# Feature-major x for two attention batches: the norm's scales and shifts go through DRAM and GpSimd

## The reference, cut to what matters

```python
def _layernorm(x, axis=-1, eps=1e-05):
    m = jnp.mean(x, axis=axis, keepdims=True)
    v = jnp.var(x, axis=axis, keepdims=True)
    return (x - m) / jnp.sqrt(v + eps)

# x: (4, 512, 256); ctx_1024: (4, 512, 256); 16 heads of 64, a causal window of 64
qh = (q @ wq.T).reshape(b, l, H, DH)          # q is _layernorm(x)
kh = (k @ wk.T).reshape(b, l, H, DH)          # k and v are ctx_1024
scores = jnp.einsum('bhqd,bhkd->bhqk', _rope(qh), _rope(kh)) * DH ** (-0.5)
probs = jax.nn.softmax(jnp.where(window_mask, scores, -1e+30), axis=-1)
x = x + jnp.tanh(g_xattn[0]) * (out @ wo.T)
x = x + jnp.tanh(g_ffn[0]) * ffn(_layernorm(x))   # 2 shared and 16 routed experts
```

## Time and profile before

| what | value |
|---|---|
| median of 3 runs | 520.59 us (520.58 to 520.6) |
| the profiled execution's own time | 520.59 us |
| its span in the trace | 518.8 us |
| busy in the span: PE, DVE, ACT, POOL | 504.1 (97%), 362.3 (70%), 311.1 (60%), 256.4 us (49%) |
| granted PE clock | full in all 40 slices |

### The profile page before, as it was taken

How to read it: one execution, slowest core, us unless ns; L and a number is a source line. 1 busy time by engine, 2 the same in 40 slices (tenths; PEclk the granted TensorE clock), 3 DMA queues, 4 the chain that set the end, 5 groups by cost and what they waited for, 6 DMA issues and landing times.

```text
span 518.8 us, 12294 instructions
## 1 busy us (share of the span) xinstructions
PE 504.1 (97%) x4394; PEld 422.6 (81%) x4394; DVE 362.3 (70%) x1165; ACT 311.1 (60%) x859; POOL 256.4 (49%) x198
## 2 busy tenths in 40 slices
PE   8888999899999999999999999999999999999997
PEld 5767798799889989888888888777887888788885
DVE  6868868658756677785978586797657665855454
ACT  3468677466675657756685794774546545544442
POOL 4999997788889778987987730101000100000000
PEclk9999999999999999999999999999999999999999
DMA  7361222111031011201212119314911491166021
GB/s 258 99 170 53 76 77 103 58 37 37 4 118 37 8 33 37 59 7 53 57 42 58 37 50 322 103 31 117 296 23 22 125 287 17 23 153 232 1 33 48
DMA packets 47723, 44.12 MB, mean 85 GB/s; under 512 B 29168, under 2 KB 31472, under 8 KB 47664
## 3 DMA queue, kind: packets, MB, share of 16 engines
q1 hardware_dynamic: 47664, 43.35, 29.8%
HBM read 30.62 MB, written 2.23 MB: 63 GB/s over the span
## 4 chain that ended last, share of the span: by engine, by line
PE 75%; POOL 10%; DVE 7%; issue 4%; ACT 2%; DMA 1%; SPq 0%; DVEq 0%; POOLq 0%; ACTq 0%
PE ring L1017 53%; PE psS L1017 10%; PE psO L1199 4%; PE psT L1180 4%; PE psS L1168 4%; POOL arena L465 3%; POOL arena L467 2%; POOL prob L471 2%; DVE arena L772 1%; POOL wl L479 1%; DVE wl L848 1%; DVE arena L918 1%; POOL arena L458 1%; DVE arena L775 1%; DMA craw<-in_ctx 1%
## 5 line engine op out<-in xcount | busy, mean ns | idle before, releaser
L1017 PE MATMUL ring<-xTh,wh 128*128 128x512 f32 x272 | 110.0, 404 | 1.8 <-DVE wl L848 1.5
L1017 PE MATMUL ring<-xTh,wl 128*128 128x512 f32 x272 | 106.8, 393 | 0.0
L1017 PE MATMUL ring<-xTl,wh 128*128 128x512 f32 x272 | 106.7, 392 | 0.0
L471 POOL TENSOR_TENSOR prob<-prob,rinv 128x512 f32<-128x512 f32 x64 | 68.4, 1069 | 19.4 <-DVE rinv L928 19.4
L566 ACT ACTIVATE oTh<-prob 128x512 fp32r<-128x512 f32 x64 | 40.4, 631 | 54.3 <-PE ring L1017 25.9
L831 DVE TENSOR_TENSOR oTl<-prob,oTh 128x512 fp32r<-128x512 f32 x64 | 43.9, 687 | 35.6 <-ACT oTh L566 35.1
L1017 PEld LDWEIGHTS ring<-xTh,wh 128*128 128x128 f32 x272 | 51.1, 188 | 14.9 <-issue 2.9
L550 ACT ACTIVATE sneg<-ring 128x512 f32<-128x512 f32 x72 | 42.9, 596 | 33.6 <-PE ring L1017 33.5
L490 POOL TENSOR_TENSOR rstd<-vare,mhalf 128x4 f32<-128x4 f32 x8 | 10.1, 1267 | 103.3 <-DVE vare L741 103.3
L641 ACT ACTIVATE pT<-psT 128x512 f32<-128x512 f32 x64 | 38.0, 594 | 38.2 <-PE psT L1180 38.2
L1017 PEld LDWEIGHTS ring<-xTh,wl 128*128 128x128 f32 x272 | 51.1, 188 | 11.3
(11 more groups left out here) (123 smaller groups left out, 1227.5 us busy)
## 6 DMA issues: line engine op xcount, KB each, us to landing
arena<-gate_scratch SPq DMA_DIRECT2D x64, 256.0 KB, 6.5
raw<-in_e SPq DMA_DIRECT2D x18, 256.0 KB, 2.7
raw<-in_w SPq DMA_DIRECT2D x16, 256.0 KB, 3.5
arena<-arena SPq DMA_DIRECT2D x16, 256.0 KB, 3.1
arena<-arena SPq DMA_DIRECT2D x16, 192.0 KB, 3.5
pT<-pT SPq DMA_DIRECT2D x96, 32.0 KB, 2.0
out<-x SPq DMA_DIRECT2D x16, 128.0 KB, 6.0
x<-in_x SPq DMA_DIRECT2D x3, 512.0 KB, 3.7
```

The lines of the kernel that those rows point to most:

```text
L471: pool.tensor_tensor(prob[:, c % BUFS, :, :], prob[:, c % BUFS, :, :], rinv[:, c % BUFS, :].unsqueeze(2).to_broadcast([P, TT, P]), ALU.mul ...
L1017: last = pe.matmul(out, a, b, start=start and i == 0 and j == 0, stop=stop and i == n - 1 and j == 2, skip_group_check=check)
```

## The change

For the batches 2 and 3 (the third and the fourth), x is also loaded from DRAM with the features on the partitions, into the tile `xn` that the normalised x took before. The scale (`rstd`) and shift of each token lie one token to a partition; SP writes them to a DRAM scratch and reads them back spread over all partitions, first the scales and later the shifts, into the tile `idle`. POOL multiplies and adds (two halves each, 128x512). ACT rounds the result to `xTh[0]`, DVE subtracts to `xTl[0]` in two halves. Batch 1 keeps the old way; so do all norms of the experts. The statistics of batches 2 and 3 move from step (k, g) = (3, 1) to step (0, 0) of the batch before.

```diff
+        xd = xn[:, :, :].rearrange("p t d -> p (t d)").rearrange("p (k n) -> p k n", k=KC)
+        xd_tiles = xd.rearrange("p k (t c) -> p k t c", t=TT)
+        by_tile = idle.rearrange("p (c t) -> p t c", t=TT)
+        norm_d = nc.dram_tensor("norm_scratch", (B, 2, L), F32).ap()
...
-            if (k, g) == (2, 2) and b + 1 < B:
-                jobs.append(("xT", b + 1))
-            if (k, g) == (3, 1) and b + 1 < B:
-                jobs.append(("stat", b + 1))
+            if (k, g, b) == (2, 2, 0):
+                jobs.append(("xT", 1))
+            if (k, g, b) == (3, 1, 0):
+                jobs.append(("stat", 1))
+            spread = {(0, 0): "stat", (1, 0): "norm_out", (2, 0): "in_scale", (3, 0): "scale_a", (0, 1): "scale_b",
+                      (1, 1): "in_shift", (3, 1): "shift_a", (0, 2): "shift_b", (2, 2): "xhi_d", (3, 2): "xlo_d"}
+            if 1 <= b < B - 1 and (k, g) in spread:
+                jobs.append((spread[k, g], b + 1))
...
-            if (k, g) == (0, 2) and b + 1 < B:
-                jobs.append(("norm_a", b + 1))
-            if (k, g) == (1, 2) and b + 1 < B:
-                jobs.append(("norm_b", b + 1))
+            if (g, b) == (2, 0) and k < 2:
+                jobs.append(("norm_a" if k == 0 else "norm_b", 1))
...
@@ @block.sync
+                elif kind == "norm_out":
+                    sp.wait_ge(ln_rstd, n + 1)
+                    for i, part in enumerate((rstd, shift)):
+                        sp.dma_start(norm_d[n, i].rearrange("(p t) -> p t", t=TT), part[:, :]).then_inc(norm_out, 16)
+                    if n == 2:
+                        sp.wait_ge(xT_pe, 2)
+                    else:
+                        sp.wait_ge(xT_lo, n)
+                    sp.dma_start(xd, xt_d[n]).then_inc(in_xt, 16)
+                elif kind == "in_scale":
+                    sp.wait_ge(norm_out, 32 * (n - 1))
+                    if n > 2:
+                        sp.wait_ge(x_shifted, n - 2)
+                    sp.dma_start(idle, norm_d[n, 0].partition_broadcast(P)).then_inc(in_scale, 16)
+                elif kind == "in_shift":
+                    sp.wait_ge(x_scaled, n - 1)
+                    sp.dma_start(idle, norm_d[n, 1].partition_broadcast(P)).then_inc(in_shift, 16)
...
@@ @block.gpsimd
+                elif kind in ("scale_a", "scale_b"):
+                    kc = int(kind == "scale_b")
+                    pool.wait_ge(in_xt, 16 * (n - 1))
+                    pool.wait_ge(in_scale, 16 * (n - 1))
+                    scaled = pool.tensor_tensor(xd_tiles[:, kc, :, :], xd_tiles[:, kc, :, :], by_tile, ALU.mult)
+                    if kc:
+                        scaled.then_inc(x_scaled, 1)
+                elif kind in ("shift_a", "shift_b"):
+                    kc = int(kind == "shift_b")
+                    pool.wait_ge(in_shift, 16 * (n - 1))
+                    moved = pool.tensor_tensor(xd_tiles[:, kc, :, :], xd_tiles[:, kc, :, :], by_tile, ALU.add)
...
                 elif kind == "stat":
                     pool.wait_ge(ln_stat, n + 1)
...
@@ @block.scalar
+                elif kind == "xhi_d":
+                    act.wait_ge(x_shifted, n - 1)
+                    act.wait_ge(qk_pe[0], GROUPS * n + 1)
+                    act.activation(xTh[0][:, :, :], xd, ACT.Copy).then_inc(xT_hi, 1)
...
@@ @block.vector
+                elif kind in ("xhi_d", "xlo_d"):
+                    kc = int(kind == "xlo_d")
+                    dve.wait_ge(xT_hi, n + 1)
+                    rest = dve.tensor_tensor(xTl[0][:, kc, :], xd[:, kc, :], xTh[0][:, kc, :].bitcast(F32),
+                                             ALU.subtract)
```

More of the change, by code:

```diff
@@ L59, in products, with build @@
     return ((sh, mh), (sh, ml), (sl, mh))
-def build(nc, x_d, ctx_d, gx_d, gf_d, w_d, e_d, rw_d, cos_d, sin_d, mask_d, ident_d, out_d):
+def build(nc, x_d, xt_d, ctx_d, gx_d, gf_d, w_d, e_d, rw_d, cos_d, sin_d, mask_d, ident_d, out_d):
     with ExitStack() as ctx:
@@ L160, in build @@
         ln_norm = sem("ln_norm")
+        norm_out, in_xt, in_scale, in_shift = sem("norm_out"), sem("in_xt"), sem("in_scale"), sem("in_shift")
+        x_scaled, x_shifted = sem("x_scaled"), sem("x_shifted")
         xT_pe, xT_hi, xT_lo = sem("xT_pe"), sem("xT_hi"), sem("xT_lo")
@@ L289, in released, with by_pe @@
                     "r": (r_sub, n + 1)}[kind]
+        def by_pe(j):
+            return j if j < 2 else j - B + 2
         def fillings(u):
@@ L485, in do @@
                                        ALU.subtract).then_inc(c_lo, 1)
+                elif kind in ("scale_a", "scale_b"):
[9 more added lines that the diff above has]
+                    moved = pool.tensor_tensor(xd_tiles[:, kc, :, :], xd_tiles[:, kc, :, :], by_tile, ALU.add)
+                    if kc:
+                        moved.then_inc(x_shifted, 1)
                 elif kind == "stat":
                     pool.wait_ge(ln_stat, n + 1)
-                    if n:
-                        pool.wait_ge(ln_norm, n)
+                    if n in (3, 4):
+                        pool.wait_ge(norm_out, 32 * (n - 2))
+                    elif n:
+                        pool.wait_ge(ln_norm, by_pe(n - 1) + 1)
                     power = pool.tensor_tensor(rstd[:, :], vare[:, :], mhalf[:, :], ALU.pow)
@@ L534, in round_bank_pair @@
             def round_bank_pair(dst, job, ready, done):
-                act.wait_ge(ready, job[1] + 1)
+                act.wait_ge(ready, by_pe(job[1]) + 1)
                 two = banks(job)
@@ L617, in normalise @@
                 act.wait_ge(ln_rstd, j + 1)
-                act.wait_ge(xT_pe, min(j, B + 2))
+                if j == 1:
+                    act.wait_ge(xT_pe, 1)
+                elif j == B:
+                    act.wait_ge(xT_lo, B)
+                else:
+                    act.wait_ge(xT_pe, by_pe(min(j, B + 2)))
                 if j > B + 2:
@@ L880, in do @@
                     last.then_inc(gT_out, 1)
+                elif kind in ("xhi_d", "xlo_d"):
[3 more added lines that the diff above has]
+                                             ALU.subtract)
+                    if kc:
+                        rest.then_inc(xT_lo, 1)
                 elif kind == "turn":
-                    dve.wait_ge(ln_norm, B + n + 1)
+                    dve.wait_ge(ln_norm, by_pe(B + n) + 1)
                     dve.wait_ge(z_out, 4 * (n - 1))
@@ L1099, in do @@
                         pe.wait_ge(in_ident, 16)
-                    pe.wait_ge(ln_norm, n + 1)
+                    pe.wait_ge(ln_norm, by_pe(n) + 1)
                     for kc in range(KC):
@@ L1287 @@
     xt = a(x).reshape(B, TT, P, D).transpose(0, 2, 1, 3)
+    xd = a(x).reshape(B, L, KC, P).transpose(0, 3, 2, 1)
     ct = a(ctx_1024).reshape(B, L, KC, P).transpose(0, 3, 2, 1)
@@ L1302 @@
     cos, sin, mask, ident = tables()
-    arrays = dict(x=xt, ctx=ct, gx=a(g_xattn), gf=a(g_ffn), w=w, e=e, rw=rw, cos=cos, sin=sin,
+    arrays = dict(x=xt, xt=xd, ctx=ct, gx=a(g_xattn), gf=a(g_ffn), w=w, e=e, rw=rw, cos=cos, sin=sin,
                   mask=mask, ident=ident)
```

## The result

The changed kernel takes 528.18 us in the median of 5 runs (526.8 to 530.59), the kernel before beside it 520.58 us (520.17 to 520.6): a ratio of 1.0152, with a 95% interval of 1.0124 to 1.0179. It is slower by 7.6 us. The time lies 1.7 us above the 526.5 forecast and inside the range. Its executions spread by 3.8 us where those of before spread by 0.4; that spread turned out to be part of the answer.

The account below looks back on a forecast made before the run. PE was taken as the bound from 100 to 200 us, with POOL the feeding engine with least room. The sum was 520.59 + 7.86 for two waits - 1.96 for removed transposes = 526.5 us, range 524.6 to 530.5.

Parts of the forecast that it names:

- The place and the mechanism: Steps 16 and 32: POOL waits for `vare` before `rotate_q`, delaying divides that PE needs; 2 x 3.93 = 7.86 us.
- The wait: PE at the transposes of head 16, and alike at head 32, stands 3.63 us for POOL's late divide.
- DVE's 2.56 us for the statistics: DVE's statistics, begun at 101.34 in step 16, take 2.56 us as in step 23 before, giving `vare` at 103.90.
- The second wait: PE at head 17's transposes waits 0.30 us more for `divide(17)`; 3.93 us together with the first wait.
- The branch that had the mechanism right: The forecast as worked out, POOL's wait for `vare` reaching PE twice: 525.3 to 527.4 us, chance 0.55.
- the dear operand: Rival: scaling and shifting exceed POOL's idle places, by slow operation or late landing; 0.5 to 2.2 us a batch, 527.5 to 531, chance 0.25.
- The saving: Two sets of eight transposes removed from PE save 0.87 + 1.09 = 1.96 us.
- the operations on POOL: Four new 128x512 operations per batch, 1.3 us each, just fit POOL's idle places and cost zero.
- The 0.55 us a batch: By the skill's step rule, POOL's operations take 1.97 us, not 1.3; after the slack some 0.55 us a batch, 1.1 in sum.
- The spreads of scales and shifts: SP's DMAs: the scales' spread lands 6.5 us after issue, at 117.8 before POOL wants it at 118.3; zero cost.
- DVE's lateness: DVE, about 2 us late with the keys' rotation and maxima, has caught up by `y(3)`, since PE is later.

Follow-up runs that it names:

- The statistics alone, moved: Kernel before, with only the statistics of batches 2 and 3 moved to step (0, 0) of the batch before, on DVE and POOL: 530.41 us, ratio 1.0188.
- the run with PE kept at work: Changed kernel plus three 128x512 matrix products on PE ahead of the transposes of heads 16 and 32: 526.47 us, ratio 1.0109.
- the doubled run: Kernel with statistics one step earlier, plus a second same-shape operation behind each of POOL's eight new ones, into an unread tile: 529.68 us, ratio 1.0162.
- the run in which POOL's wait alone was cured: Kernel before, with DVE's statistics moved to step (0, 0) but POOL's power and product left in old step (3, 1): 527.28 us, ratio 1.0126.
- POOL's part two steps later: Changed kernel with DVE's statistics still in step (0, 0), POOL's power and product moved to step (2, 0), behind the rotations: 537.56 us, ratio 1.0316.

## Why the prediction was right, point by point

**The place and the mechanism** were right: POOL waits for `vare` ahead of `rotate_q(5)` and `rotate_q(9)`, and PE waits for the divides behind them. The statistics alone, moved, reproduce it (3.15 us at heads 16 and 32); placed ahead of the rotation or one step earlier, the wait is gone.

**The wait** was worked out as 3.63 and is 3.16 in the ledger, in three traces (3.15 and 3.16). The term at fault is DVE's 2.56 us for the statistics. In the changed kernel they take 104.67 - 102.59 = 2.08:

```profile
102.59 1.39 DVE L787 BATCH_NORM_STATS2 stats<-x 128x6 f32<-128x256 f32 x4
...
104.43 0.17 DVE L793 TENSOR_SCALAR nmean<-mv 128x4 f32<-128x4 f32 x1
104.51 0.16 DVE L794 TENSOR_SCALAR vare<-mv 128x4 f32<-128x4 f32 x1
```

The small product `nmean` took 0.66 in step 23 of the kernel before, where it ended with POOL's divide (127.53 and 127.50), 2.08 with POOL in its rotation, and 0.17 here, where POOL is idle because it waits for this very result. A duration read in a place where POOL worked was carried to one where it stands.

**The second wait**, 0.30 at head 17, is 0.28 at full clock. In the changed kernel's trace it is covered by the slow product before it.

**The clock** was missing. No term of the sum and no rival had it, though the forecast itself put PE idle for 3.6 us. It costs 2.71 and 1.55 us in the profiled execution and about 2.2 in the median, and it differs between executions: those with a mean granted clock of 0.989, 0.994 and 0.997 took 530.59, 528.0 to 528.3 and 526.8 us. At full clock the sum would be 2 x (3.16 + 0.28 + 0.08) - 1.78 = 5.3, the 0.08 being what head 18 adds in the run with PE kept at work, against the 5.9 forecast and the 5.65 measured in that run. So two errors partly cancel: the waits, less the saving, were worked out 0.3 to 0.6 us too high, and some 2.2 us for the clock were left out.

**Luck.** The range took the time in, but not for this reason. The branch that had the mechanism right, 525.3 to 527.4, does not hold 528.18; it falls into 527.5 to 531, which was kept for the dear operand. By the time alone one would have blamed POOL's new operations. Only the traces and the runs, in which those operations are all there and the kernel takes 519.3 or 519.51, tell the two apart.

**The saving** was worked out as 0.87 + 1.09 = 1.96 and is 0.80 + 0.98 = 1.78. The first 0.87 comes at once (head 24), and some 0.1 is given back by head 27.

**What is hidden**: the operations on POOL take 1.55 us, not 1.3, and cost nothing, since 1.07 us are left after them. The Trainium skill's rule on the step ("GPSIMD Engine Reference", "Performance pitfalls for Q7 kernels") gives half as much again; here it was a fifth, 1.56 against 1.29. The 0.55 us a batch that the forecast made of that rule do not come out of its own terms either: two operations longer by 0.67 make 1.34, of which the slack of 1.25 leaves 0.1. The spreads of scales and shifts landed 3.4 us after their issue in the median, not 6.5. The rival of the dear operand is refused for this kernel. An estimate of where it would begin comes from the doubled run, where 3.1 us more made POOL 1.3 too late: at 1.8 us more for the two scales, 2.4 us each in place of 1.55.

**What was right only under the other wait**: DVE's lateness was called made good by the time of `y(3)`, since PE is later than that. In the changed kernel this is so: oTl is ready at 109.58 and `y(3)` begins at 112.66. But it holds only while PE stands for POOL, and I took it for slack of DVE's own when I expected nothing of the run in which POOL's wait alone was cured. That run came out 6.5 us above the kernel before beside it.

## What to carry to other kernels

A step put earlier in one engine's list is put ahead of all that stands behind it: ask when its input will be there, and let it stand ahead of something that waits for the same engine anyway. Here one step earlier, in DVE's gap before `y`, turns a loss of 1.5% into a gain of 0.3%. Where a wait is found, look for a second one under it before you count what its cure brings, and ask whether the cure makes that one longer: here an estimated 0.5 us became 2.3, with POOL at work beside DVE. And where a change makes a busy PE stand for some us, allow for work at half clock behind it: here 1.6 to 2.7 us behind a wait of 3.0.

## What the runs showed of the hardware

- PE, at full clock and busy before, stood for 3.0 us at two places of the changed kernel, and the granted clock fell to 0.50 at both (from 111.07 to 117.90 and from 189.58 to 192.99 us). Of the four waits of 2.3 us, in the runs with DVE's part alone and with POOL's part later, two were followed by a fall (110.33 and 111.04) and two were not (185.80 and 191.89). No wait of 1.9 us or less, in any trace here from 20 to 300 us, was. How long the fall lasted differed between the two places of one trace, and the mean granted clock differed between executions of one kernel (0.989 to 0.997). A wait filled with useless products, 0.42 us left idle, left it at 1.00.
- A DVE product of 128x4 (`nmean`) took 0.17 us wherever POOL was idle, and 0.3 to 2.1 wherever it began while POOL was in an operation. In each of those places it ended 0.02 to 0.03 us after POOL's operation did; 2.08 was beside one of 128x1024.
- A product on POOL whose second operand has a step of 16 bytes took 1.56 us (128x512), without it 1.29.
- In the kernel with 1,024 writes of single elements, PE stopped for 0.82 and 1.30 us without a releaser, and a load of 512 KB issued behind the writes landed after 12.1 us and not 4.7. The cause of the stops stays open.
